# Two iota tables of a graph layer's one-hots, read by VectorE from PSUM instead of SBUF

## The chip, the cores and the metric

The kernel runs on one core of a Trainium2 chip. The metric is the device time of one execution in microseconds (us). Engines are named as in the profile: PE (TensorE matmuls), PEld (TensorE weight loads), DVE (VectorE), ACT (ScalarE), POOL (GpSimd), SP (SyncE). SBUF is the on-chip working memory, PSUM the accumulator memory that TensorE writes.

## The reference

There are 12,500 nodes with 128 features each, 200,000 edges sorted by destination, and four edge types. All tensors are float32.

```python
h = jnp.maximum(_layernorm(x, axis=-1), 0.0)
xs = h[src]
for i in range(4):
    msgs = msgs + jnp.where((edge_types == i)[:, None], xs @ W[i] + b[i], 0.0)
out = x + jax.ops.segment_sum(msgs, dst, num_segments=12500)
```

The destinations are drawn as 12500 times the square of a uniform number, so low nodes receive more edges than high ones. Because the edges are sorted, a run of 1,024 consecutive edges falls on few tiles of 128 nodes.

## The kernel before

**The table.** In the first stage (98 tiles of 128 nodes) the kernel normalizes x, applies relu, transposes on PE (L656), multiplies by all four weight matrices at once (L665), lets DVE add the bias (L524, which reads ps_y from PSUM and bias from SBUF), and stores the 128x512 result to a table in HBM (L280). A row of 128 numbers of that table is the message of one (node, type). The stage also transposes the index lists into columns: table_row (which row of the table an edge needs) and dst_col (its destination as a float). `ps_i`, one PSUM bank, takes these transposes.

**Early edges.** While the table is made, POOL gathers the raw x rows of the first 15,360 edges with 120 indirect DMAs of 128 rows (L330) into early_x. The list of rows is read from src_col in SBUF.

**The main loop.** The edges are cut into superblocks of 8 columns of 128 edges. After the table is complete, POOL gathers messages for the other superblocks with 1,443 indirect DMAs of 128 rows (L338, `gather`, called at L345). Each reads its 128 row numbers from row_stage in SBUF, which ACT fills (L407) when PE has released one of four slots (L715). POOL runs through these gathers in order and does nothing else.

For each superblock and each node tile that it touches (a pair; 294 in all) DVE makes one-hot matrices in two halves of four columns (L593): an entry is 1 where node_iota + tile_base[j] equals the edge's destination. The loop bounds come from memory (L229). PE multiplies the one-hots with the messages (L710) into ps_sum, and DVE adds the previous pair's sum to acc (L585, acc from SBUF, ps_sum from PSUM). There is one onehot buffer of two halves, so DVE may write a half again only when PE has read it (half_free, L592); PE waits for onehot_ready (L708) and for the slot's gathers (L705).

Once in nine superblocks an early one is worked off (`early=True`): DVE then also makes four one-hots of node and type together, 128x1024 each (L603, from key_iota, tile_base and key_col; the profile names their target y, whose memory they use), and PE sums normalized features by type (L737) and counts (L728) and multiplies by the weights (L746). The order of superblocks is fixed by the program: eight from the table, then one early, 15 times, then the rest.

Both `scalar_tensor_tensor` calls have three inputs: a tensor in0 (the iota), a tensor in1 (the edges' column, repeated along the nodes), and a number for each partition (tile_base) that also lies in SBUF. node_iota is 128x128 and key_iota 128x512, both made by POOL at the start (L312, L316).

Of the kernel before, what the change touches and what calls it, by code (L numbers as in the profile page):

```python
# [29 lines left out]
P = 128  # L30
# [11 lines left out]
def gnn_program(nc, x, src, dst, etype, w, b, out, table):  # L42
# [3 lines left out]
    ydim = n_types * d  # L46
# [21 lines left out]
    def sb(name, shape, dt=F32):  # L68
        return nc.alloc_sbuf_tensor(name, shape, dt)

    def ps(name, shape):
        return nc.alloc_psum_tensor(name, shape, F32)

    def sem(name):
        return nc.alloc_semaphore(name)
# [6 lines left out]
    node_iota = sb("node_iota", [P, P])  # L82
    tile_base = sb("tile_base", [P, node_tiles])
    key_iota = sb("key_iota", [P, n_types, P])
# [60 lines left out]
    ps_y = ps("ps_y", [P, 2, 512])  # L145
    ps_sum = ps("ps_sum", [P, 2, 512])
    ps_i = ps("ps_i", [P, 4, P])

    loaded_src0 = sem("loaded_src0")
    loaded_first = sem("loaded_first")  # L150
# [7 lines left out]
    own_steps = sem("own_steps")  # L158
    pads_set = sem("pads_set")
    dve_consts = sem("dve_consts")  # L160
    early_f_ready = sem("early_f_ready")
    early_transposed = sem("early_transposed")
    early_cols = sem("early_cols")
# [54 lines left out]
    def halves(tiles):  # L218
        return (0, -(-tiles // 2)), (-(-tiles // 2), tiles)
# [6 lines left out]
    def load_range(eng, s):  # L226

        regs = [eng.alloc_register(f"{eng.engine.name}_{n}_{nc.next_id()}") for n in ("lo", "hi")]
        eng.reg_load(regs, flat_ranges[0:1, bass.ds(s * 4, 2)])  # L229
        return (eng.snap(regs[0], min_val=0, max_val=node_tiles - 1),  # L230
                eng.snap(regs[1], min_val=1, max_val=node_tiles), regs)
# [14 lines left out]
    with nc.Block() as block:  # L246
# [198 lines left out]
        def _(dve):  # L445
# [88 lines left out]
            for m, op in enumerate((ALU.min, ALU.max)):  # L534
# [18 lines left out]
            dve.wait_ge(consts, 8)  # L553
            nc.vector.scalar_tensor_tensor(out=key_col[:, :], in0=type_col[:, :], scalar=float(type_step),
                                           in1=dst_col[:, 0, 0:early_tiles], op0=ALU.mult, op1=ALU.add).then_inc(own_steps, 1)
            dve.wait_ge(own_steps, 8)
            dve.wait_ge(ranges_ready, 16)
            for k in range(Y_SLOTS):
# [8 lines left out]
            nc.vector.tensor_reduce(store_after[:, :], last_touch[:, :, :], AX.X, ALU.max).then_inc(store_after_ready, 1)  # L567
            dve.wait_ge(early_gathered, 16 * early_tiles)
            dve.sem_inc(key_onehot_free, 2)

# [7 lines left out]
            def add_sums(q):  # L580
                tile = tile_before()
                dve.wait_ge(pair_added, q + 1)
                dve.wait_ge(half_free, q * 2 + 2)
                at = flat_acc[:, bass.ds(tile * d, d)]
                return nc.vector.tensor_tensor(at, at, ps_sum[:, bass.ds((q + 1) % 2, 1), 0:d], ALU.add)  # L585

            def superblock(s, tiles, early=False):
                lo, hi, regs = load_range(dve, s)
                with dve.Fori(lo, hi) as j:
                    q = count()  # L590
                    for half, (a, z) in enumerate(halves(tiles)):
                        dve.wait_ge(half_free, q * 2 + (half + 1))  # L592
                        nc.vector.scalar_tensor_tensor(  # L593
                            out=onehot[:, a:z, :],
                            in0=node_iota[:, :].unsqueeze(1).broadcast_to([P, z - a, P]),
                            scalar=tile_base[:, bass.ds(j, 1)],
                            in1=flat_dst[:, bass.ds(s * SB_TILES + a, z - a)].unsqueeze(2).broadcast_to([P, z - a, P]),
                            op0=ALU.add, op1=ALU.is_equal).then_inc(onehot_ready, 1)
                    if early:
                        p = early_count()  # L600
                        for u in range(tiles // 2):
                            dve.wait_ge(key_onehot_free, p * (tiles // 2) + (u + 1))
                            nc.vector.scalar_tensor_tensor(  # L603
                                out=key_onehot[:, u % 2, :, :],
                                in0=key_iota[:, :, :].rearrange("p t n -> p (t n)").unsqueeze(1).broadcast_to([P, 2, ydim]),
                                scalar=tile_base[:, bass.ds(j, 1)],
                                in1=key_col[:, bass.ds(s * SB_TILES + 2 * u, 2)].unsqueeze(2).broadcast_to([P, 2, ydim]),
                                op0=ALU.add, op1=ALU.is_equal).then_inc(key_onehot_ready, 1)
                        dve.reg_add(p_reg, p_reg, 1)
                    add_sums(q).then_inc(pair_added, 1)  # L610
                    dve.reg_mov(before_reg, j)
                    dve.reg_add(q_reg, q_reg, 1)

                dve.wait_ge(pair_added, count() + 1)
                dve.sem_inc(sbs_passed, 1)
                for r in regs:
                    dve.free_register(r)

            with dve.Fori(0, EARLY_SBS) as i:
                s = EARLY_SBS + i * (EARLY_ROUNDS * SLOTS)  # L620
                superblock(s, SB_TILES)

                for t in range(SB_TILES):
                    nc.vector.bn_stats(e_stats[:, t, :], flat_early[:, bass.ds((i * SB_TILES + t) * d, d)]).then_inc(e_stats_taken, 1)
                dve.wait_ge(e_stats_taken, (i + 1) * SB_TILES)
                dve.wait_ge(e_used, i + 1)
                nc.vector.tensor_tensor(
                    type_mask[:, :, 0:n_types], node_iota[:, 0:n_types].unsqueeze(1).broadcast_to([P, SB_TILES, n_types]),
                    type_col[:, bass.ds(i * SB_TILES, SB_TILES)].unsqueeze(2).broadcast_to([P, SB_TILES, n_types]),
                    ALU.is_equal).then_inc(e_mask_ready, 1)  # L630
                for t in range(SB_TILES):
                    nc.vector.bn_aggr(e_mean_var[:, t, :], e_stats[:, t, :]).then_inc(e_mean_var_ready, 1)
                superblock(s + 1, SB_TILES)
                dve.wait_ge(e_std_ready, i + 1)
                nc.vector.reciprocal(e_rstd[:, :], e_std[:, :]).then_inc(e_rstd_ready, 1)
                dve.wait_ge(e_rstd_ready, i + 1)
                nc.vector.scalar_tensor_tensor(out=e_shift[:, :], in0=e_mean_var[:, :, 0], scalar=-1.0,
                                               in1=e_rstd[:, :], op0=ALU.mult, op1=ALU.mult).then_inc(e_norm_ready, 1)
                for m in range(2, EARLY_ROUNDS * SLOTS):
                    superblock(s + m, SB_TILES)  # L640
                superblock(i, SB_TILES, early=True)
# [150 lines left out]
```

## Time and profile before

| | |
|---|---|
| Runs | 2638.77 us median of 3 (2616.4, 2638.77, 2645.23) |
| Span of the profiled execution, first to last instruction | 2029.2 us |
| Median less that span | 609.6 us |
| POOL busy | 1536.1 us, 76% |
| PE busy | 1116.0 us, 55% |
| DVE busy | 714.7 us, 35% |
| ACT busy | 169.6 us, 8% |

The span is that of one profiled execution. Its time around the span is not listed by itself, so the median less the span stands for it. Busy time counts instructions that run on an engine's data path; waits, branches and the issue of DMAs by a queue are not in it, but an indirect DMA on POOL is an instruction of POOL, since POOL makes its descriptors. "Idle before" is the time in which an engine stood still ahead of an instruction, with what ended it; "issue" means that nothing the profile shows held it.

### The profile page before, as it was taken

To read this page: it belongs to the slowest core of one execution; us is meant where nothing else is said; L and a number is where in the kernel's file an instruction comes from. 1 tells how busy PE (TensorE), PEld (TensorE's weight loads), DVE (VectorE), ACT (ScalarE), POOL (GpSimd) and SP (SyncE) were. 2 spreads that over 40 slices of the span, in tenths; PEclk is the share of its full clock that TensorE was granted. 3 is DMA by queue.
4 is the path that set the end of the run, shared out by engine and by line. 5 is a ranking of instruction groups with operands and counts; after the bars stand their busy time and mean duration, and the time that the engine had idled before them with its cause. 6 is when DMAs were issued, how large, how long until landed. Compare 5 with 4: busy or idle time off the path is not lost.

```text
span 2029.2 us, 24251 instructions
## 1 busy us (share of the span) xinstructions
PE 1116.0 (55%) x5394; PEld 930.4 (46%) x5395; DVE 714.7 (35%) x1589; ACT 169.6 (8%) x565; POOL 1536.1 (76%) x1575
## 2 busy tenths in 40 slices
PE   6952545456564554654646556456555555554555
PEld 2322444344454444544535455445544444444554
DVE  6862223132332332433424334243322222232333
ACT  4530011010010100101001001010000000000000
POOL 7777777777777777777777777777777777777775
PEclk9985767776665776767878767787777777787788
DMA  9962221212122112211212121211312222212222
GB/s 305 328 206 54 51 52 50 53 49 52 51 50 52 50 49 52 51 51 49 50 52 50 50 52 50 51 50 50 104 51 70 51 51 52 69 51 52 69 52 59
DMA packets 94959, 144.09 MB, mean 71 GB/s; under 512 B 27065, under 2 KB 57267, under 8 KB 94947
## 3 DMA queue, kind: packets, MB, share of 16 engines
q0 software_dynamic: 50016, 102.53, 19.8%
q1 hardware_dynamic: 40537, 39.02, 5.8%
q10 hardware_dynamic: 4394, 2.40, 0.4%
q8 instruction: 4, 0.07, 0.0%
q14 instruction: 8, 0.07, 0.0%
HBM read 111.76 MB, written 32.09 MB: 71 GB/s over the span
## 4 chain that ended last, share of the span: by engine, by line
POOL 70%; issue 24%; PE 3%; DMA 1%; POOLq 1%; DVE 0%; ACT 0%; DVEq 0%; ACTq 0%; PEldq 0%
POOL messages L338 65%; POOL early_x L330 6%; PE ps_sum L710 2%; DMA messages<-message_table,row_stage 1%; PE ps_y L737 1%; PE ps_y L728 0%; POOLq L342 0%; POOLq L344 0%; DMA src_rows<-in_src 0%; PE ps_sum L746 0%; POOLq L345 0%; DVE onehot L593 0%; POOLq L246 0%; ACT row_stage L407 0%; DVE acc L585 0%
## 5 line engine op out<-in xcount | busy, mean ns | idle before, releaser
L338 POOL DMA_INDIRECT messages<-message_table,row_stage x1443 | 1420.5, 984 | 439.7 <-issue 437.9
L710 PE MATMUL ps_sum<-messages,onehot 128*128 128x128 f32 x4438 | 843.4, 370 | 852.9 <-DMA messages<-message_table,row_stage 769.7
L710 PEld LDWEIGHTS ps_sum<-messages,onehot 128*128 128x128 f32 x4438 | 791.0, 277 | 904.5 <-issue 890.5
L593 DVE SCALAR_TENSOR_TENSOR onehot<-node_iota,tile_base,dst_col 128x512 f32<-128x512 f32 x586 | 431.1, 749 | 1234.2 <-PE ps_sum L710 1147.0
L407 ACT COPY row_stage<-table_row 128x8 int32 (+2 forms) x181 | 35.7, 198 | 1602.5 <-PEq L715 1597.8
L330 POOL DMA_INDIRECT early_x<-in_x,src_col x120 | 113.5, 946 | 41.6 <-issue 39.4
L665 PE MATMUL ps_y<-w_sb,h_t 128*128 128x512 f32 x196 | 104.7, 626 | 4.6 <-DVE y L524 4.3
L737 PE MATMUL ps_y<-y 128*128 128x512 f32 x240 | 106.8, 598 | 0.0
L603 DVE SCALAR_TENSOR_TENSOR y<-key_iota,tile_base,key_col 128x1024 f32<-128x1024 f32 x60 | 75.9, 1285 | 35.5 <-PE ps_y L737 35.5
L585 DVE TENSOR_TENSOR acc<-acc,ps_sum x294 | 82.1, 279 | 2.3 <-PE ps_sum L710 2.1
L524 DVE TENSOR_TENSOR y<-ps_y,bias 128x512 f32<-128x512 f32 x98 | 66.9, 684 | 16.5 <-PE ps_y L665 11.4
L737 PEld LDWEIGHTS ps_y<-y 128*128 128x128 f32 x240 | 42.8, 193 | 53.5 <-issue 36.3
L372 ACT ACTIVATE h<-acc,shift,rstd 128x128 f32 (+1 forms) x97 | 48.3, 498 | 0.6 <-DVE shift L473 0.2
L425 ACT ACTIVATE y<-early_x,e_shift,e_rstd 128x128 f32 x120 | 48.1, 484 | 0.0
L665 PEld LDWEIGHTS ps_y<-w_sb,h_t 128*128 128x128 f32 x196 | 29.7, 191 | 36.4 <-issue 33.6
L728 PE MATMUL ps_y<-onehot,type_mask 128*128 128x128 f32 x240 | 35.9, 311 | 18.9 <-DVE onehot L593 18.9
L728 PEld LDWEIGHTS ps_y<-onehot,type_mask 128*128 128x128 f32 x240 | 32.8, 219 | 22.4 <-DVE onehot L593 22.4
L656 PE MATMUL ps_t<-ident,h 128*128 128x128 f32 x98 | 27.7, 284 | 11.7 <-ACT h L384 9.8
L656 PEld LDWEIGHTS ps_t<-ident,h 128*128 128x128 f32 x98 | 14.0, 143 | 39.8 <-issue 26.2
L746 PEld LDWEIGHTS ps_sum<-w_sb,bias 128*128 128x128 f32 x120 | 14.5, 191 | 30.2 <-issue 30.2
L397 ACT COPY h_t<-ps_t 128x128 f32<-128x128 f32 x98 | 25.8, 263 | 30.1 <-PE ps_t L656 29.4
L746 PE MATMUL ps_sum<-w_sb,bias 128*128 128x128 f32 x120 | 17.3, 287 | 17.9 <-ACT edge_counts L435 17.9
(63 smaller groups left out, 147.5 us busy)
## 6 DMA issues: line engine op xcount, KB each, us to landing
message_table<-y SPq DMA_DIRECT2D x98, 256.0 KB
messages<-message_table,row_stage POOLq DMA_INDIRECT x1443
out<-acc SPq DMA_DIRECT2D x6, 896.0 KB
acc<-in_x SPq DMA_DIRECT2D x4, 896.0 KB, 7.5
early_x<-in_x,src_col POOLq DMA_INDIRECT x120
acc<-in_x ACTq DMA_DIRECT2D x2, 896.0 KB, 10.3
acc<-in_x SPq DMA_DIRECT2D x1, 832.0 KB, 6.9
src_rows<-in_src SPq DMA_DIRECT2D x1, 640.0 KB
```

The source lines that it names most:

```text
L330: pool.indirect_dma_start(early_x[:, t, :], None, x, bass.IndirectOffsetOnAxis(ap=src_col[:, t:t + 1], axis=0)).then_inc(early_gathered, 16)
L338: pool.indirect_dma_start(messages[:, k, t, :], None, table_rows, bass.IndirectOffsetOnAxis(ap=row_stage[:, k, t:t + 1], axis=0)).then_inc ...
L372: nc.scalar.activation(h[:, k, :], flat_acc[:, bass.ds(n * d, d)], ACT.Relu, bias=flat_shift[:, bass.ds(n, 1)], scale=flat_rstd[:, bass.ds ...
L425: nc.scalar.activation(e_h[:, t, :], flat_early[:, bass.ds((i * SB_TILES + t) * d, d)], ACT.Relu, bias=e_shift[:, t:t + 1], scale=e_rstd[: ...
L524: nc.vector.tensor_tensor(y[:, i % Y_SLOTS, :], ps_y[:, i % 2, :], bias[:, :], ALU.add).then_inc(y_ready, 1)
L585: return nc.vector.tensor_tensor(at, at, ps_sum[:, bass.ds((q + 1) % 2, 1), 0:d], ALU.add)
L593: nc.vector.scalar_tensor_tensor(out=onehot[:, a:z, :], in0=node_iota[:, :].unsqueeze(1).broadcast_to([P, z - a, P]), scalar=tile_base[:, ...
L603: nc.vector.scalar_tensor_tensor(out=key_onehot[:, u % 2, :, :], in0=key_iota[:, :, :].rearrange("p t n -> p (t n)").unsqueeze(1).broadcas ...
L665: nc.tensor.matmul(ps_y[:, i % 2, :], h_t[:, i % 2, :], w_flat, start=True, stop=True).then_inc(y_done, 1)
L710: ins = nc.tensor.matmul(ps_sum[:, bass.ds(q % 2, 1), 0:d], onehot[:, t, :], messages[:, k, t, :], start=(t == 0), stop=(t == tiles - 1))
L728: ins = nc.tensor.matmul(ps_y[:, 1, 0:P], type_mask[:, t, :], onehot[:, t, :], start=(t == 0), stop=(t == SB_TILES - 1))
L737: ins = nc.tensor.matmul(ps_y[:, 0, :], e_h[:, 2 * u + t, :], key_onehot[:, u % 2, t, :], start=(u == 0 and t == 0), stop=(u == SB_TILES / ...
```

## The change

Two PSUM tensors are filled once, ahead of the main loop, with copies of node_iota and key_iota: `ps_node` is new, and `ps_key` is another name for the bank `ps_i`, whose last reader (the copy of type_col, L550) stands before it on DVE. The one-hots of L593 and L603 read in0 from there. The other two inputs, the output, the shapes and the order stay. `type_mask` (L627) still reads node_iota from SBUF.

```diff
--- before.py
+++ after.py
@@ -145,6 +145,8 @@
     ps_y = ps("ps_y", [P, 2, 512])
     ps_sum = ps("ps_sum", [P, 2, 512])
     ps_i = ps("ps_i", [P, 4, P])
+    ps_node = ps("ps_node", [P, P])
+    ps_key = ps_i[:, :, :].rearrange("p t n -> p (t n)")
 
     loaded_src0 = sem("loaded_src0")
     loaded_first = sem("loaded_first")
@@ -158,6 +160,7 @@
     own_steps = sem("own_steps")
     pads_set = sem("pads_set")
     dve_consts = sem("dve_consts")
+    iotas_in_psum = sem("iotas_in_psum")
     early_f_ready = sem("early_f_ready")
     early_transposed = sem("early_transposed")
     early_cols = sem("early_cols")
@@ -553,6 +556,8 @@
             dve.wait_ge(consts, 8)
             nc.vector.scalar_tensor_tensor(out=key_col[:, :], in0=type_col[:, :], scalar=float(type_step),
                                            in1=dst_col[:, 0, 0:early_tiles], op0=ALU.mult, op1=ALU.add).then_inc(own_steps, 1)
+            nc.vector.tensor_copy(ps_node[:, :], node_iota[:, :]).then_inc(iotas_in_psum, 1)
+            nc.vector.tensor_copy(ps_key, key_iota[:, :, :].rearrange("p t n -> p (t n)")).then_inc(iotas_in_psum, 1)
             dve.wait_ge(own_steps, 8)
             dve.wait_ge(ranges_ready, 16)
             for k in range(Y_SLOTS):
@@ -567,6 +572,7 @@
             nc.vector.tensor_reduce(store_after[:, :], last_touch[:, :, :], AX.X, ALU.max).then_inc(store_after_ready, 1)
             dve.wait_ge(early_gathered, 16 * early_tiles)
             dve.sem_inc(key_onehot_free, 2)
+            dve.wait_ge(iotas_in_psum, 2)
 
 
 
@@ -592,7 +598,7 @@
                         dve.wait_ge(half_free, q * 2 + (half + 1))
                         nc.vector.scalar_tensor_tensor(
                             out=onehot[:, a:z, :],
-                            in0=node_iota[:, :].unsqueeze(1).broadcast_to([P, z - a, P]),
+                            in0=ps_node[:, :].unsqueeze(1).broadcast_to([P, z - a, P]),
                             scalar=tile_base[:, bass.ds(j, 1)],
                             in1=flat_dst[:, bass.ds(s * SB_TILES + a, z - a)].unsqueeze(2).broadcast_to([P, z - a, P]),
                             op0=ALU.add, op1=ALU.is_equal).then_inc(onehot_ready, 1)
@@ -602,7 +608,7 @@
                             dve.wait_ge(key_onehot_free, p * (tiles // 2) + (u + 1))
                             nc.vector.scalar_tensor_tensor(
                                 out=key_onehot[:, u % 2, :, :],
-                                in0=key_iota[:, :, :].rearrange("p t n -> p (t n)").unsqueeze(1).broadcast_to([P, 2, ydim]),
+                                in0=ps_key.unsqueeze(1).broadcast_to([P, 2, ydim]),
                                 scalar=tile_base[:, bass.ds(j, 1)],
                                 in1=key_col[:, bass.ds(s * SB_TILES + 2 * u, 2)].unsqueeze(2).broadcast_to([P, 2, ydim]),
                                 op0=ALU.add, op1=ALU.is_equal).then_inc(key_onehot_ready, 1)
```

## Rows read from the trace of the kernel before

**Rows 1.** The page: span, busy time by engine, and the chain that ended last

```profile
span 2029.2 us, 24251 instructions
PE 1116.0 (55%) x5394; PEld 930.4 (46%) x5395; DVE 714.7 (35%) x1589; ACT 169.6 (8%) x565; POOL 1536.1 (76%) x1575
...
POOL 70%; issue 24%; PE 3%; DMA 1%; POOLq 1%; DVE 0%; ACT 0%; DVEq 0%; ACTq 0%; PEldq 0%
```

**Rows 2.** Waits: engine, tile and line, releaser: us in total, times, longest

```profile
DVE onehot L593 <- PE ps_sum L710: 1147.0, 432, 9.2
...
PE ps_sum L710 <- DMA messages<-message_table,row_stage: 769.7, 140, 37.9
POOL messages L338 <- issue: 437.9, 1437, 0.3
...
POOL messages L338 <- ACT row_stage L407: 1.8, 6, 0.3
```

**Rows 3.** Groups by line, POOL: count | busy us, mean ns | idle before

```profile
L338 POOL DMA_INDIRECT messages<-message_table,row_stage x1443 | 1420.5, 984 | 439.7 <-issue 437.9 <-ACT row_stage L407 1.8
```

**Rows 4.** Single lines, L338 and L330: durations in ns, minimum/median/maximum

```profile
L338 POOL DMA_INDIRECT messages<-message_table,row_stage x1443: 940/944/1554, 158.3 to 2017.3; - x181
...
L330 POOL DMA_INDIRECT early_x<-in_x,src_col x120: 940/944/1103, 5.1 to 157.1; - x120
```

**Rows 5.** Timeline, main loop: start us, us, engine, line

```profile
1433.07 1.22 POOL L338 DMA_INDIRECT messages<-message_table,row_stage  x1 [0.30 <-issue]
...
1437.09 1.42 POOL L338 DMA_INDIRECT messages<-message_table,row_stage  x1 [0.30 <-issue]
...
1432.73 0.75 DVE L593 SCALAR_TENSOR_TENSOR onehot<-node_iota,tile_base,dst_col 128x512 f32<-128x512 f32 x1 [0.77 <-PE ps_sum L710]
...
1436.28 1.41 DVE L593 SCALAR_TENSOR_TENSOR onehot<-node_iota,tile_base,dst_col 128x512 f32<-128x512 f32 x2 [2.61 <-issue]
```

**Rows 6.** Timeline, an early superblock: a gather beside L603

```profile
907.35 2.48 DVE L603 SCALAR_TENSOR_TENSOR y<-key_iota,tile_base,key_col 128x1024 f32<-128x1024 f32 x2
907.89 1.55 POOL L338 DMA_INDIRECT messages<-message_table,row_stage  x1 [0.30 <-issue]
```

**Rows 7.** Timeline, table stage: an early gather beside L524

```profile
65.24 0.94 POOL L330 DMA_INDIRECT early_x<-in_x,src_col  x1 [0.30 <-issue]
...
64.41 1.42 DVE L524 TENSOR_TENSOR y<-ps_y,bias 128x512 f32<-128x512 f32 x2
```

**Rows 8.** Groups by line and shape, DVE: count | busy us, mean ns | idle before

```profile
L593 DVE SCALAR_TENSOR_TENSOR onehot<-node_iota,tile_base,dst_col 128x512 f32<-128x512 f32 x584 | 430.3, 751 | 1232.8 <-PE ps_sum L710 1145.5 <-issue 54.0 <-PE ps_sum L748 31.9
L603 DVE SCALAR_TENSOR_TENSOR y<-key_iota,tile_base,key_col 128x1024 f32<-128x1024 f32 x60 | 75.9, 1285 | 35.5 <-PE ps_y L737 35.5
L524 DVE TENSOR_TENSOR y<-ps_y,bias 128x512 f32<-128x512 f32 x98 | 66.9, 684 | 16.5 <-PE ps_y L665 11.4 <-DMA message_table<-y 4.6
...
L593 DVE SCALAR_TENSOR_TENSOR onehot<-node_iota,tile_base,dst_col 128x128 f32<-128x128 f32 x1 | 0.3, 350 | 0.2 <-PE ps_sum L710 0.2
...
L554 DVE SCALAR_TENSOR_TENSOR key_col<-type_col,dst_col 128x120 f32<-128x120 f32 x1 | 0.3, 282 | 0.0
```

**Rows 9.** Groups by line and shape, the late stretch 1420 to 2018 us

```profile
L338 POOL DMA_INDIRECT messages<-message_table,row_stage x466 | 456.7, 980 | 142.0 <-issue 141.7 <-ACT row_stage L407 0.3
...
L710 PE MATMUL ps_sum<-messages,onehot 128*128 128x128 f32 x1750 | 314.3, 354 | 286.2 <-DMA messages<-message_table,row_stage 276.7 <-issue 2.7 <-DVE onehot L593 2.5
...
L585 DVE TENSOR_TENSOR acc<-acc,ps_sum x109 | 30.4, 279 | 0.0
```

**Rows 10.** Timeline, between table stage and main loop, and the end

```profile
135.03 0.28 DVE L554 SCALAR_TENSOR_TENSOR key_col<-type_col,dst_col 128x120 f32<-128x120 f32 x1
...
136.15 2.92 DVE L564 SCALAR_TENSOR_TENSOR y<-ranges,order 1x196 f32<-1x196 int32 x7 [0.84 <-DMA ranges<-ranges_by_chunk]
...
161.47 1.41 DVE L593 SCALAR_TENSOR_TENSOR onehot<-node_iota,tile_base,dst_col 128x512 f32<-128x512 f32 x2 [20.80 <-issue]
...
2017.31 0.95 POOL L338 DMA_INDIRECT messages<-message_table,row_stage  x1 [0.30 <-issue]
```

## The prediction

> **What bounds the kernel now.** I read the page first: POOL is busy for 76% of the span, PE for 55%, DVE for 35%, and the chain that ended last lies on POOL for 70% and on "issue" for 24% [rows 1]. The waits say what that issue is: 437.9 us in 1,437 pieces of at most 0.3 us ahead of the gathers of L338, so POOL's own pause between two gathers. Only 1.8 us of POOL's idle time waited for a list of rows from ACT, while PE waited 769.7 us for gathered data and DVE 1147.0 us for PE [rows 2]. From 158.3 us to the start of the last gather at 2017.3 us the kernel runs at the pace at which POOL issues gathers, and the end follows about 11 us later (2029.2 less 2018.3, where the last gather ends) [rows 1, 10]. DVE and PE have spare time; what counts is what they do to POOL.
>
> The third view, the durations of that one line, shows it. The gathers are all alike (128 rows of 512 bytes), the minimum is 940 ns and the median 944 ns, yet the maximum is 1554 [rows 4] and the mean 984 [rows 3]. Something stretches a minority. The timeline shows what. The gather at 1433.07 took 1.22 us, and the one-hot of L593 that ran beside it ended at 1432.73 + 0.75 = 1433.48. The gather at 1437.09 took 1.42 us; of the two one-hots in a row beside it, 1.41 us in all, the end is at 1436.28 + 1.41 = 1437.69 [rows 5]. End of the one-hot, less start of the gather, less the gather's excess over 0.944: 0.41 - 0.28 = 0.13 us and 0.60 - 0.48 = 0.12 us. So each gather reaches, some 0.12 us after its start, a point that it does not pass while that one-hot runs; after it everything takes the usual 0.82 us. L603 does the same to the gather at 907.89, which took 1.55 us [rows 6]: the first of its two instructions ends near 907.35 + 1.28 = 908.63, and 0.74 - 0.61 = 0.13. A gather reads its 128 row numbers from SBUF, and both one-hots read two SBUF tensors, the iota and the edge column.
>
> **Whether one PSUM input frees POOL.** The row for that is L524, whose in0 is in PSUM and in1 (bias) in SBUF, the arrangement that the change gives to L593 and L603. It takes 67 us of the table stage [rows 8], beside the early gathers, which also read row numbers from SBUF. The gather at 65.24 passes its point at 65.36 while two L524 run until 64.41 + 1.42 = 65.83, and takes 0.94 us; with the stretch above it would have taken 1.41 [rows 7]. In all 120 early gathers the median is 944 and the maximum 1103 [rows 4], although L524 covers about 67 of their 153 us. So the stretch goes with two SBUF tensors, not with any DVE work. What L524 lacks is the third input: tile_base, one number per partition, also from SBUF. No row has one SBUF tensor with such a number, so this stays the main doubt (a rival below).
>
> **The change, part by part.**
> (1) Gathers. Removed: 1443 x (984 - 944) = 57.7 us [rows 3, 4]. All of it is on the chain, since POOL is never idle but for its 0.3 us pauses. Bounds: nothing, if the third input keeps the stretch, and 1443 x (984 - 940) = 63.5, if every gather became the fastest. I take 57.7, because L524's neighbours show the median as their usual duration. A few two-input instructions are left (L627, L637); they are short and rare.
> (2) The one-hot's own duration. A one-hot takes 751 ns for 512 columns and 350 for 128 [rows 8], so (751 - 350) / 384 = 1.04 ns a column and 217 ns fixed. L554, the same operation with a constant instead of tile_base, has 282 - 125 = 157 fixed; tile_base so costs 60 ns. L524, 512 columns with one PSUM input, takes 684. Estimate for the new form: 684 + 60 = 744, no change. Bounds: 684 ns below, and above 1285, the price of 1024 columns now, if PSUM gave a column only every second cycle [rows 8]. I take 744, for L524 reads PSUM at the full rate while PE writes other banks. The Trainium skill, "VectorE: DVE Perf Modes", section on the TRN2 errata, speaks against the change: it gives VectorE 58 cycles plus the columns from SBUF and 120 from PSUM. By that, an estimate from the page, each one-hot would be 62 cycles or 65 ns longer, 42 us of DVE time over 644; L524's row, no longer than a two-SBUF form, does not show it. By either, the sum here hides it under POOL: in the late stretch PE still waits 276.7 us for gathers in 109 pairs, 2.5 us a pair [rows 9], and a pair has two one-hots. Even at the upper bound, 2 x 0.53 = 1.07 us fit in there. Without that cover a pair would pay those 1.07 us, 315 us in 294 pairs.
> (3) The two copies. 512 columns for about L524's 684 ns and 128 for about L554's 282, together 1.0 us (bounds 0.5 and 1.6, half of it and L603's 1285 with the 128-column one-hot's 350). They stand behind L554, which ends at 135.31; DVE then waits 0.84 us for the ranges anyway, and after L564 and its reduce it idles 20.80 us before the first one-hot at 161.47, until the early gathers have landed [rows 10]. Behind them on DVE are only L564 and the table for the output stores, used some 100 us later. The added wait for both copies stands behind the wait for the early gathers. Cost: zero. If that cover were gone, 1 us. No copy or wait is put on POOL, SP, ACT or PE, and no DMA is moved.
> (4) What is late next. Still POOL: 944 + 304 (437.9 / 1437) = 1.25 us a gather. Rows come early: the longest wait of POOL for ACT is 0.3 us [rows 2]. At 8 gathers a superblock, POOL's new pace is 9.98 us; in the late stretch (466 gathers, 58 superblocks, 109 pairs [rows 9]) PE's 314.3 us are 5.4 us a superblock. PE keeps up, and its waits shrink.
> Sum: -57.7 + 0 + 0. The profiled span would be 2029.2 - 57.7 = 1971.5 us. With the 609.6 us around it the profiled execution stands, as far as can be told, at the median, so 2638.8 - 57.7 = 2581 us, 2.2% less. The three runs lie from 22 us below the median to 6 above; taking 1% as the least that can be told from no change is taking 26 us.
>
> **Rivals.**
> *A. The stretch stays* (the change does not do what it is thought to). tile_base is a second SBUF input, and if POOL's read is shut out by any two of them, nothing moves: 2639 us. For it: no row excludes it. Against: the number is one column, and its visible price is 60 ns; if it shut POOL out only for those, the stretch per hit would fall to under a tenth. A middle case, half of the stretch left, gives 2610.
> *B. DVE becomes the bound.* The place is the pair: one-hot half, four matmuls, half free. If PSUM gave the repeated 128-column iota at a quarter of the rate, a one-hot would take 0.22 + 4 x 0.53 = 2.35 us instead of 0.75, two of them 3.2 us more in a pair. PE's wait of 2.54 us a pair, less what POOL saves (57.7 / 294 = 0.20), covers 2.34; 0.86 us x 294 = 253 us are left, and the time is 2581 + 253 = 2834. It decides from 0.75 + 2.34 / 2 = 1.9 us a one-hot. Against: L524 reads 512 columns in 684 ns; for: L524's PSUM columns are all different, and no row rereads the same 128.
> *C. The gain is there and something else takes part of it*: gathers in closer order land later, or PE waits more at the early superblocks, where its work is longest. The 1.8 us of POOL's waiting [rows 2] would grow; at 20 us the time is 2601.
>
> **How the numbers follow.** Forecast 0.72; A 0.11 (and its middle case 0.05); B 0.03; C 0.09. The predicted time is the forecast's, 2581. Its own range is the sum's bound of 63.5 and the runs' spread, 2555 to 2602. C and half of the middle case belong into 8 in 10, so the high end goes to 2615; the low end stays at 2555. Faster by over 1% (below 2612) takes the forecast, C and half of the middle case: 0.83. Within 1%: A and the rest, 0.14. Slower: 0.03.
>
> **What would show it right or wrong.** Right: L338's mean falls from 984 to about 945 with the median unchanged and a maximum near 1100; its busy time falls from 1420.5 to about 1363; the pauses stay at 304 ns; POOL's wait for ACT stays under 5 us; the one-hots stay within 684 to 820 ns; PE's wait for gathers falls below 770 us; the last gather starts near 1960. A: mean at 984 and gathers that still end a fixed time after a one-hot. B: one-hots of 1.9 us and more, and POOL waiting for row_stage. C: the mean falls and the wait of POOL for ACT grows. The forecast is wrong in its frame if the span falls by 58 us and the runs do not.

## The result

The changed kernel takes 2667.12 us (median of 4, 2656.13 to 2669.64), the kernel before 2627.59 us beside it (median of 4, 2614.0 to 2645.23). The ratio is 1.0193, 95% interval 1.0137 to 1.0249: slower by 1.9%, where 2.2% faster was forecast.

The page of the changed kernel, to be held against [rows 1]:

```profile
span 2667.7 us, 24253 instructions
PE 1224.0 (46%) x5394; PEld 995.8 (37%) x5395; DVE 717.6 (27%) x1591; ACT 169.1 (6%) x565; POOL 1476.9 (55%) x1575
...
another core or an unknown queue 40%; PE 24%; issue 21%; DVE 7%; DVEq 7%; PEld 1%; ACT 0%; DMA 0%; ACTq 0%; PEldq 0%; SPq 0%
```

The span is 638.5 us longer than in the profile of before, although POOL is busy for 59 us less and the chain no longer lies on POOL. This execution took 2669.64 us in all, 2 us more than its span. So there are no 600 us around a span here, and the profiled execution of before must have been another case than the runs that were listed beside it; e1 below tests that. Its groups answer to [rows 3] and [rows 8]:

```profile
L341 POOL DMA_INDIRECT messages<-message_table,row_stage x1443 | 1361.4, 943 | 1125.5 <-ACT row_stage L410 668.5
...
L599 DVE SCALAR_TENSOR_TENSOR onehot<-ps_node,tile_base,dst_col 128x512 f32<-128x512 f32 x586 | 434.4, 749 | 1652.7 <-remote 938.1
...
L609 DVE SCALAR_TENSOR_TENSOR y<-ps_i,tile_base,key_col 128x1024 f32<-128x1024 f32 x60 | 75.1, 1279 | 125.2 <-remote 83.5
```

The durations of the gathers, as [rows 4] had them:

```profile
L341 POOL DMA_INDIRECT messages<-message_table,row_stage x1443: 938/944/961, 265.9 to 2643.4; - x181
```

Every stretched gather is gone: the longest takes 961 ns and took 1554. The one-hots keep their duration (for 512 columns 750 ns and before 751, for 1024 columns 1279 and 1285; the 749 above also counts two smaller ones). But the gathers begin at 265.9 us instead of 158.3 and end 626 us later than they did. The waits, beside [rows 2], say where the time is:

```profile
ACT row_stage L410 <- PEq L721: 1607.5, 131, 30.4
...
DVE onehot L599 <- remote: 938.1, 151, 20.0
POOL messages L341 <- ACT row_stage L410: 668.5, 84, 108.5
PE ps_sum L716 <- DVE onehot L599: 506.4, 114, 14.7
POOL messages L341 <- issue: 457.0, 1359, 3.4
```

POOL waited 1.8 us for lists of rows, now 668.5. "remote" is a release that no recorded event explains. A stretch of the timeline shows what such a wait is:

```profile
1033.80 2.05 PE L716 MATMUL ps_sum<-messages,onehot 128*128 128x128 f32 x16 [1.53 <-issue]
...
1035.11 0.75 DVE L599 SCALAR_TENSOR_TENSOR onehot<-ps_node,tile_base,dst_col 128x512 f32<-128x512 f32 x1 [1.74 <-issue]
...
1040.42 0.75 DVE L599 SCALAR_TENSOR_TENSOR onehot<-ps_node,tile_base,dst_col 128x512 f32<-128x512 f32 x1 [4.57 <-remote]
1040.50 0.20 ACT L410 COPY row_stage<-table_row 128x8 int32 x1 [7.82 <-PEq L721]
```

PE ends its last matmul at 1035.85. DVE waits for that matmul's semaphore (half_free) and goes on at 1040.42; ACT, which gets its release through PE, at 1040.50. The signal is about 4.5 us late, and both stand still for it while POOL goes on gathering. It is so in the table stage too, which the change does not touch. Here are ACT's copies of the transposes there:

```profile
32.80 0.27 ACT L400 COPY h_t<-ps_t 128x128 f32<-128x128 f32 x1 [7.74 <-issue]
...
40.50 0.27 ACT L400 COPY h_t<-ps_t 128x128 f32<-128x128 f32 x1 [7.05 <-remote]
...
49.60 0.27 ACT L400 COPY h_t<-ps_t 128x128 f32<-128x128 f32 x1 [8.44 <-issue]
```

In the profile of before, such copies follow each other at about 1 us there. I call these **late signals**. The same trace shows what they go with. POOL's last early gather starts at 156.4 us. Of the 98 copies of this line, 18 start between 20 and 170 us, while gathers run or have just ended, and 76 in the 95 us behind that, when POOL issues none (one at 183.33 us, for example, and the next at 184.38).

In the profile of before the early gathers run just as close together, and all 98 copies are made by 129.5 us. So dense gathers alone do not make signals late everywhere; in this execution they are late while gathers are issued.

### The profile page after: what moved, and what is told of

Read it like the earlier page. It is cut to its first block, busy times and chain, and to the rows that moved or that the text cites. A ratio compares the mean times of both kernels' runs of the same rounds, so it can differ in the third digit from the quotient of the medians.

```text
span 2667.7 us, 24253 instructions
## 1 busy us (share of the span) xinstructions
PE 1224.0 (46%) x5394; PEld 995.8 (37%) x5395; DVE 717.6 (27%) x1591; ACT 169.1 (6%) x565; POOL 1476.9 (55%) x1575
## 4 chain that ended last, share of the span: by engine, by line
another core or an unknown queue 40%; PE 24%; issue 21%; DVE 7%; DVEq 7%; PEld 1%; ACT 0%; DMA 0%; ACTq 0%; PEldq 0%; SPq 0%
PE ps_sum L716 16%; DVE onehot L599 3%; PE ps_y L671 3%; PE ps_y L743 3%; DVEq L232 2%; DVE acc L591 2%; DVEq L591 1%; DVEq L599 1%; PEld ps_sum L716 1%; PE ps_sum L752 1%; DVE y L609 1%; PE ps_y L734 1%; DVEq L595 1%; DVE y L527 0%
## 5 line engine op out<-in xcount | busy, mean ns | idle before, releaser
L341 POOL DMA_INDIRECT messages<-message_table,row_stage x1443 | 1361.4, 943 | 1125.5 <-ACT row_stage L410 668.5
L716 PE MATMUL ps_sum<-messages,onehot 128*128 128x128 f32 x4438 | 890.3, 381 | 1143.0 <-DVE onehot L599 506.4
L716 PEld LDWEIGHTS ps_sum<-messages,onehot 128*128 128x128 f32 x4438 | 822.8, 286 | 1209.6 <-issue 1056.7
L599 DVE SCALAR_TENSOR_TENSOR onehot<-ps_node,tile_base,dst_col 128x512 f32<-128x512 f32 x586 | 434.4, 749 | 1652.7 <-remote 938.1
L671 PE MATMUL ps_y<-w_sb,h_t 128*128 128x512 f32 x196 | 123.3, 725 | 98.3 <-issue 96.2
L743 PE MATMUL ps_y<-y 128*128 128x512 f32 x240 | 125.3, 678 | 62.7 <-DVE y L609 62.7
L609 DVE SCALAR_TENSOR_TENSOR y<-ps_i,tile_base,key_col 128x1024 f32<-128x1024 f32 x60 | 75.1, 1279 | 125.2 <-remote 83.5
L743 PEld LDWEIGHTS ps_y<-y 128*128 128x128 f32 x240 | 51.1, 229 | 127.3 <-DVE y L609 73.2
L734 PE MATMUL ps_y<-onehot,type_mask 128*128 128x128 f32 x240 | 54.6, 419 | 80.7 <-DVE onehot L599 53.9
L734 PEld LDWEIGHTS ps_y<-onehot,type_mask 128*128 128x128 f32 x240 | 50.4, 319 | 84.6 <-DVE onehot L599 56.8
```

The lines of the kernel that those rows point to most:

```text
L341: pool.indirect_dma_start(messages[:, k, t, :], None, table_rows, bass.IndirectOffsetOnAxis(ap=row_stage[:, k, t:t + 1], axis=0)).then_inc ...
L599: nc.vector.scalar_tensor_tensor(out=onehot[:, a:z, :], in0=ps_node[:, :].unsqueeze(1).broadcast_to([P, z - a, P]), scalar=tile_base[:, ba ...
L609: nc.vector.scalar_tensor_tensor(out=key_onehot[:, u % 2, :, :], in0=ps_key.unsqueeze(1).broadcast_to([P, 2, ydim]), scalar=tile_base[:, b ...
L671: nc.tensor.matmul(ps_y[:, i % 2, :], h_t[:, i % 2, :], w_flat, start=True, stop=True).then_inc(y_done, 1)
L716: ins = nc.tensor.matmul(ps_sum[:, bass.ds(q % 2, 1), 0:d], onehot[:, t, :], messages[:, k, t, :], start=(t == 0), stop=(t == tiles - 1))
L734: ins = nc.tensor.matmul(ps_y[:, 1, 0:P], type_mask[:, t, :], onehot[:, t, :], start=(t == 0), stop=(t == SB_TILES - 1))
```

## The experiments

All kernels here share one edit of SP's stores, which loads the seven store points one by one:

```diff
-            regs = [sp.alloc_register(f"sp_store_after_{n}") for n in range(len(STORE_TILES))]
-            sp.reg_load(regs, store_after[0:1, :])
...
-                sp.wait_ge(sbs_passed, sp.snap(reg, min_val=0, max_val=full_sbs + 1) + 1)
+                after = sp.value_load(store_after[0:1, n:n + 1], min_val=0, max_val=full_sbs + 1)
+                sp.wait_ge(sbs_passed, after + 1)
```

**e1, the kernel before with that edit.**

> The kernel before, with one edit that all experiments here carry: SP loads its seven store points one at a time, just ahead of each wait, instead of all at once. Theory L (late signals): the profile of before was an exceptional execution. Ordinary executions of both kernels hold pauses in which a finished matmul's semaphore reaches DVE, ACT and PE several us late, about 600 us in all. Then this run is 2600 to 2650 us, its profile shows a span within 5 us of its time, POOL waiting for ACT's row_stage for some 500 to 700 us, and hundreds of us of late signals; L338's mean is still 960 to 985 ns. Theory P (pace of POOL, as predicted): the profile shows a span near 2030 again and POOL without waits, and some 600 us lie outside the span in every run.

Measured: 2606.63 us; the kernel before beside it 2605.9 us (23 runs); ratio 1.0051 [1.0013, 1.0089]. Span and waits:

```profile
span 2638.2 us, 24271 instructions
...
DVE onehot L592 <- remote: 899.7, 156, 19.4
POOL messages L337 <- ACT row_stage L406: 578.0, 73, 108.0
```

Theory L holds. The kernel before, run again, has late signals as well; the profile that the prediction read had none. Gathers: mean 992 ns, so the stretch is there too.

**e2, the changed kernel with that edit.**

> The changed kernel with the same edit of SP. Theory L: 1.4% to 2.5% slower than before as measured, 2655 to 2675 us, and POOL's gathers at 943 ns. If the 1.9% were a matter of one chip or of the code's exact place, it shrinks below 1%.

Measured: 2657.35 us, ratio 1.0235 [1.0187, 1.0283]. The loss repeats; POOL's wait for ACT is 659.5 us.

**e3, copies only.** The one-hots read SBUF, the two copies stay:

```diff
-                            in0=ps_node[:, :].unsqueeze(1).broadcast_to([P, z - a, P]),
+                            in0=node_iota[:, :].unsqueeze(1).broadcast_to([P, z - a, P]),
...
-                                in0=ps_key.unsqueeze(1).broadcast_to([P, 2, ydim]),
+                                in0=key_iota[:, :, :].rearrange("p t n -> p (t n)").unsqueeze(1).broadcast_to([P, 2, ydim]),
```

> The changed kernel, but L593 and L603 read node_iota and key_iota from SBUF again; the two copies into PSUM stay. Theory R (the reads from PSUM cost the 1.9%, by sharing PSUM with TensorE's writes): same as before, within 0.5%, near 2630, gathers' mean back at 980. Theory F (the faster gathers cost it, through what they trigger): also same as before. Theory S (the set-up costs it: two instructions more, another length of code): 1.5 to 2% slower, near 2667.

Measured: 2610.61 us, ratio 1.0062 [1.0024, 1.0100], the same as e1; in its profile POOL waits 524.5 us for ACT. The set-up costs nothing that shows (theory S falls); the loss comes with the reads.

**e4, only L593's reads from PSUM**: e3's second pair of lines alone.

> The changed kernel, but L603 reads key_iota from SBUF; L593 (586 of 646 one-hots) reads PSUM. Theory R and F: nine tenths of the change, 1.5 to 2% slower than before. If the 128x1024 reads of L603 are what costs, in the early superblocks where PE is busiest, it is within 0.5% of before.

Measured: 2651.18 us, ratio 1.0205 [1.0156, 1.0254]; gathers' mean 958 ns. Nearly the whole loss comes with L593's reads.

**What the late signals go with.** In each trace I took the waits of DVE ahead of a one-hot of L593 (half_free) on which it stood idle for over 0.1 us, the distance from the end of the last matmul before it to DVE's start, and the number of gathers that POOL had started in the 20 us up to that matmul's end. In e1, 10 or 11 gathers: 112 waits, median 0.18 us; 12 or 13: 209, median 0.18 us (mean 1.7); 14 or 15: 78, median 3.1 us; 16 or 17: 12 waits, median 13.4 us. The other three are alike. In the profile of before, 16 or 17 gathers stand ahead of 241 waits, with a median of 0.15 us. So in e1 to e4 lateness goes with POOL's pace, and the next experiments change the pace.

**e5 to e8, pauses of POOL.** Ahead of gathers POOL clears a small tile (w columns); e5 does it once for a superblock (its `t % 8` and `t // 8` stand where the others have 1), the others for each gather:

```diff
+                    if first is not None and t % 1 == 0:
+                        pool.wait_ge(paused, first + t // 1)
+                        pool.sem_inc(slots_taken, 1)
+                        pool.memset(pause[:, :], 0.0).then_inc(paused, 1)
                     pool.indirect_dma_start(
```

e5 (changed kernel, 256 columns a superblock):

> The changed kernel with a pause of POOL ahead of each superblock's eight gathers: a memset of 128x256 and its semaphores, about 0.35 us, which is what the one-hots' stretch gave to POOL before (8 x 0.04 us). In the profiles of e1 to e4 a PE signal is the later the more gathers were issued in the 20 us before it: median 0.04 us up to 13 gathers, 3 us with 14 or 15, 11 us and more with 16. Theory F (the faster gathers cost the 1.7% between e1 and e2, since they make signals later): back near e1, 2600 to 2625 us. Theory R (reading PSUM while PE writes it costs it): stays at e2's 2657 us or above.

Measured: 2685.49 us, ratio 1.0303 [1.0249, 1.0357]. Theory F's return to 2600 does not come. Its lump ahead of eight gathers leaves them as dense among themselves, so it does not settle the matter of pace. It is 28 us slower than e2, which nothing here explains.

e6 (before, 64 columns a gather):

> The kernel before with a pause of POOL of some 0.15 to 0.25 us ahead of each gather (memset of 128x64), a pace near 1.45 us a gather instead of 1.29. Theory D (density): signals come on time when gathers are spaced, since each gather's 16 completions then no longer pile up; the late signals shrink and the kernel becomes bound by POOL at 170 + 1443 x 1.45 = 2260 to 2400 us, far faster than before. Against it (late signals belong to the chip's state, whatever the pace): 2606 plus up to 290 us, 2700 or more.

Measured: 2572.9 us, ratio 0.9790 [0.9707, 0.9873]. A slower POOL makes a faster kernel, by 2.1%, but not by what D hoped: the memset partly hid under the gathers (mean distance of two gathers 1.35 us, not 1.45), and signals stayed late.

e7 (changed, 64 columns a gather):

> The changed kernel with the same pause. Theory D with F: with signals on time POOL bounds, so the stretch that the change removes counts again, and it is 30 to 60 us faster than e6. Theory R: the PSUM reads cost 1.7% here too, so slower than e6 by some 40 us, or equal where the two offset.

Measured: 2672.12 us, ratio 1.0259 [1.0189, 1.0330], slower than e6 by 99 us. Signals are late in both, so the condition of D with F is not met; theory R has the sign, at more than twice its size.

e8 (before, 256 columns a gather):

> The kernel before with a pause near 0.35 us ahead of each gather (128x256), a pace near 1.62 us. Theory D: no late signals beyond those of the table stage; bound by POOL, 170 + 1443 x 1.62 = 2500 us (2450 to 2560), so slower than e6 and still faster than before. Against D: 2750 or more.

Measured: 2455.46 us, ratio 0.9421 [0.9359, 0.9484], 5.8% faster than the kernel before. Its waits:

```profile
DVE onehot L599 <- PE ps_sum L716: 1355.9, 354, 10.8
PE ps_sum L716 <- DMA messages<-message_table,row_stage: 1032.0, 152, 18.3
...
POOL pause L342 <- ACT row_stage L413: 106.9, 1, 106.9
```

and its groups:

```profile
L343 POOL DMA_INDIRECT messages<-message_table,row_stage x1443 | 1446.2, 1002 | 260.5 <-POOL pause L342 168.2 <-issue 92.3
...
L342 POOL MEMSET pause<- 128x256 f32 x1440 | 472.1, 328 | 107.8 <-ACT row_stage L413 106.9
```

The picture of [rows 2] is back: PE waits for gathered data, the "remote" waits of DVE have left the top of the list, and POOL waits only once, 106.9 us at the end of the table stage. The time follows as there: first gather at 264.6 us, 1443 gathers at 1.51 us, 2439 us. Theory D expected 2450 to 2560 and its rival 2750 or more: spacing the gathers makes the signals come on time here. For a kernel whose one-hots read SBUF the change comes between 1.35 us (e6) and 1.49 us a gather (e8).

**e9 to e12, meant to tell PSUM reads from the lost stretch.** Behind each one-hot DVE runs one more instruction with an unused result: e9 and e10 in e3's kernel, e11 and e12 in the changed one.

```diff
                             op0=ALU.add, op1=ALU.is_equal).then_inc(onehot_ready, 1)
+                        dve.wait_ge(junk_done, q * 2 + (half + 1))
+                        dve.sem_inc(junk_steps, 1)
+                        nc.vector.bn_stats(junk[:, :], key_iota[:, :, :].rearrange("p t n -> p (t n)")).then_inc(junk_done, 1)    # e9, e11
+                        nc.vector.bn_stats(junk[:, :], ps_key).then_inc(junk_done, 1)           # e10
+                        nc.vector.tensor_tensor(junk[:, :], key_iota[:, :, :].rearrange("p t n -> p (t n)"), key_iota[:, :, :].rearrange("p t n -> p (t n)"), ALU.add).then_inc(junk_done, 1)  # e12
```

> Control of e10: the one-hots read SBUF as before (and two SBUF tensors, so they stretch gathers), and behind every one-hot of L593 DVE runs one more instruction with a single input: statistics over 512 columns of key_iota in SBUF, about 0.65 us, 588 in all, result unused. DVE has idle time for it: within 1% of e3 (2610), or slower by what 1.3 us of DVE a pair adds to the turn of one-hot and matmuls; only the difference to e10 counts.

> As e9, but the added statistics read the copy of key_iota in PSUM: 588 reads of 512 columns of PSUM on top, the one-hots as before, the gathers stretched as before. Theory R (reading PSUM beside PE's writes delays PE's signals and costs the 1.7%): slower than e9 by 1 to 2%, 25 to 50 us. Theory T (it is the missing lock-out of POOL's reads, not PSUM, that costs): equal to e9 within 0.5%.

> The changed kernel (one-hots read PSUM, gathers unstretched) with e9's added instruction, one SBUF input, no stretch of gathers. Control of e12. Theories R and T: slower than e9 by 1.5 to 2%, as e2 is against e3.

> The changed kernel; behind each one-hot DVE adds two SBUF tensors of 512 columns (0.69 us, result unused), which brings the lock-out of POOL's reads back: gathers' mean near 980 ns again, while the one-hots still read PSUM. Theory T: the loss goes, at least 1.5% faster than e11 and near e9. Theory R: equal to e11 within 0.5%, or slower by the stretch.

These four ran on another chip, and there the kernel before took 2030.12 us (17 runs). Measured: e9 2036.8 us, ratio 1.0038 [1.0023, 1.0053]; e10 2038.01, 1.0048 [1.0030, 1.0066]; e11 1971.45, **0.9714 [0.9694, 0.9734]**; e12 2044.33, 1.0069 [1.0049, 1.0090]. So whether signals are late depends on where the kernel runs, and the profile of before, with its span of 2029.2 us, came from a case like this one. Here the forecast is right. Span and gathers of e9, then of e11:

```profile
span 2034.6 us, 25446 instructions
...
L343 POOL DMA_INDIRECT messages<-message_table,row_stage x1443 | 1426.5, 989 | 439.7 <-issue 438.5 <-ACT row_stage L412 1.2
```

```profile
span 1973.6 us, 25446 instructions
...
L343 POOL DMA_INDIRECT messages<-message_table,row_stage x1443 | 1365.0, 946 | 440.0 <-issue 436.0 <-ACT row_stage L412 4.0
L602 DVE SCALAR_TENSOR_TENSOR onehot<-ps_node,tile_base,dst_col 128x512 f32<-128x512 f32 x586 | 437.0, 746 | 843.4 <-PE ps_sum L722 724.9 <-issue 94.1 <-PE ps_sum L760 23.0
```

The gathers give back 61.5 us of POOL, the span 61.0 and the median 65.35, and little else moves: POOL's pause is 0.3 us in both, its wait for ACT at most 4 us in all. e12 against e11 is the reverse test. The added instruction has two SBUF inputs in e12 and one in e11, and takes 686 and 684 ns. With two, the kernel takes 73 us more:

```profile
L343 POOL DMA_INDIRECT messages<-message_table,row_stage x1443 | 1435.6, 995 | 439.8 <-issue 438.5 <-ACT row_stage L412 1.2
```

POOL's gathers grow by 70.6 us, and each of the 302 that are over 0.06 us longer than the median ends a fixed 0.82 us (within 0.04) after one of the added instructions ended. The added instruction of e12 also writes 512 columns where that of e11 writes 6; but e11's one-hots write 512 columns too, and no gather beside them is stretched. An added instruction with a single input costs at most 7 us (e9 against the kernel before). e10 against e9: 586 more reads of 512 columns of PSUM beside PE's writes cost nothing clear of noise where signals come on time.

**e13 to e15** ran on a third chip, with late signals (kernel before 2624.14 us, 11 runs).

> The changed kernel as in e2. Where the kernel before takes about 2030 us (signals on time): 2031 - 58 = 1973 us, 2.9% faster, L338's counterpart at 944 ns, as predicted. Where it takes about 2610 us (late signals): 2657 us, 1.8% slower, as in e2.

Measured: 2673.5 us, ratio 1.0168 [1.0123, 1.0213]; the loss once more.

e14 is e8's pause in the changed kernel:

> The changed kernel with e8's pause ahead of each gather (1.45 us a gather instead of e8's 1.51). Signals on time: bound by POOL, 170 + 1443 x 1.45 = 2265 us. Late placement: if the change only ever acts through POOL's pace and 1.45 still spaces the completions enough, 2455 - 82 = 2373 us; if 1.45 is already too dense (e6 at 1.41 took 2573), 2500 to 2600; if reading PSUM itself delays signals, more than 2600.

Measured: 2532.57 us, ratio 0.9617 [0.9568, 0.9666]; e8 had 0.9421. Neither 2373 nor above 2600. Waits and gathers:

```profile
DVE onehot L605 <- remote: 715.8, 186, 10.6
...
POOL pause L345 <- ACT row_stage L416: 240.4, 32, 108.3
...
L346 POOL DMA_INDIRECT messages<-message_table,row_stage x1443 | 1372.2, 951 | 269.3 <-issue 176.2 <-POOL pause L345 93.1
```

Late signals return. The gathers are 51 ns shorter than e8's, which may be enough; but the one-hots also read PSUM here and SBUF in e8, and the two ran on different chips, so the record does not say which of these brings them back.

> As e12: one-hots read PSUM, an added two-SBUF-input instruction behind each brings the lock-out of POOL back. Late placement: theory T (the missing lock-out costs) 2600 to 2630 us, like e1; theory R (reads of PSUM cost) 2650 us or more, like e2. Signals on time: 2044 us as in e12.

Measured: 2712.6 us, ratio 1.0329 [1.0286, 1.0372]. Theory T expected 2600 to 2630 and gets no support; theory R's 2650 or more is met. But the added instruction also lengthens DVE's part of each pair, and no control for that ran on such a chip.

**e16 to e18** are e9, e10 and e11 again, meant as those controls; they ran on a fourth chip, where signals are on time (before 2031.73 us, 11 runs).

> As e9 (one-hots read SBUF, lock-out of POOL as before, one added single-input DVE instruction reading SBUF behind each one-hot). Late placement: the added 0.69 us stands in the turn of one-hot and matmul, so 1 to 2% slower than before: ratio 1.01 to 1.02. Signals on time: 1.004 as in e9.

> As e10, the added instruction reads PSUM. Late placement: theory R (reads of PSUM delay signals) at least 1% slower than e16; if it equals e16 within 0.5%, PSUM reads as such cost nothing, and the loss hangs on POOL's gathers coming closer together. Signals on time: equal to e16.

> As e11 (one-hots read PSUM, no lock-out, added single-input instruction). Late placement: theory T (the missing lock-out costs) slower than e15's ratio of 1.033, or at least 1.5% slower than e16; with theory R alone it equals e15. Signals on time: 0.971 as in e11.

Measured: ratios 1.0048 [1.0032, 1.0064], 1.0044 [1.0029, 1.0059] and 0.9708 [0.9694, 0.9721]. They confirm e9 to e11 and leave the question of e15 open.

**All paces together**, on the chips with late signals. Pace is the mean distance between the starts of two gathers in the profiled execution, without the distances over 3 us, in which POOL waited:

| run | one-hots read | pace us | profiled execution us | median us | ratio to before |
|---|---|---|---|---|---|
| changed kernel | PSUM | 1.276 | 2670 | 2667 | 1.0193 |
| e13 | PSUM | 1.276 | 2680 | 2674 | 1.0168 |
| e2 | PSUM | 1.277 | 2660 | 2657 | 1.0235 |
| e5 | PSUM | 1.287 | 2686 | 2685 | 1.0303 |
| e4 | PSUM (L593) | 1.289 | 2666 | 2651 | 1.0205 |
| e15, added instruction | PSUM | 1.293 | 2722 | 2713 | 1.0329 |
| e7 | PSUM | 1.307 | 2663 | 2672 | 1.0259 |
| e1 | SBUF | 1.322 | 2640 | 2607 | 1.0051 |
| e3 | SBUF | 1.324 | 2593 | 2611 | 1.0062 |
| e6 | SBUF | 1.349 | 2597 | 2573 | 0.9790 |
| e14 | PSUM | 1.446 | 2537 | 2533 | 0.9617 |
| e8 | SBUF | 1.493 | 2452 | 2455 | 0.9421 |

Where the one-hots read SBUF, the time falls as the gathers are spaced. Where they read PSUM, it does not follow the pace below 1.31 us, and falls only in e14.

Measured as above, waits in which DVE started over 2 us after the matmul's end: 152 in e1 with 934 us in all, 150 in e2 with 918, 143 in e6 with 992, 164 in e14 with 740, 5 in e8 with 18, and 7 each in e9 (46 us) and e11 (44), which gather every 1.29 and 1.25 us on a chip with signals on time. So the sum tells the two regimes apart, but not one late run from another: e6 has more of it than e1 and is faster.

Another difference of the late traces is PE's granted clock, 0.666 over the changed kernel's profile and 0.758 over that of before; PE's work takes 1224.0 us there and 1116.0 here. These 108 us are far less than the 638.5, and a slower matmul does not explain a DVE that goes on 4.5 us after its end. Which of the two brings the other was not tested.

## Why the prediction was wrong

**The step that failed is its frame**: "With the 609.6 us around it the profiled execution stands, as far as can be told, at the median". The step put 609.6 us outside the span; the runs show 2 us there (2667.7 and 2669.64 in the changed kernel, 2638.2 and 2640.11 in e1). The runs listed were, judging by e1, executions with late signals; the profile was one without. A bottleneck read from that trace, POOL, was applied to runs in which POOL stands waiting for 578 us (e1). The prediction had the warning in its own table, 600 us that nothing accounted for, and named the failure at its end ("the span falls by 58 us and the runs do not"), but gave it no chance of its own.

**Step 1, the gathers, was right in size, and wrong about the chain.** 1443 x (984 - 944) = 57.7 us was forecast for POOL. POOL's gathers fell by 61.5 us from e9 to e11, and by 76 us from e3 to e2 (1437.1 to 1361.2). On the chips with signals on time, that is the whole story: 2.9% faster, 58.7 us (e11) and 59.5 us (e18) under the kernel before, with one DVE instruction more behind each one-hot; the changed kernel by itself ran on no such chip. The main doubt, whether tile_base keeps the lock-out (the holding up of gathers beside a one-hot), is settled there: it does not. On the late chips the 76 us turned into waiting, and more: POOL's wait for ACT rose by 135 us, from 524.5 (e3) to 659.5 (e2). That the stretch ends at a fixed point holds beyond the three gathers that the prediction worked out: in the profile of before 183 gathers are over 0.06 us longer than the median, and each ends within 0.04 us of the end of an L593 or L603 plus 0.82 us.

**Step 2, the one-hot's duration: right.** 744 ns was estimated, 750 (changed kernel) and 746 (e11) measured. The Trainium skill's 62 more cycles for a PSUM source (VectorE: DVE Perf Modes, the section on the TRN2 errata) would have made it, by estimate, some 816; no run here shows them. The statistics added in e9 and e10 are the plainer test, one operation on 512 columns from either memory: 687 ns from SBUF and 692 from PSUM.

**Step 3, the copies: right.** 288 and 684 ns, 1.0 us forecast; e3 shows no cost clear of noise.

**Step 4, what is late next, failed with the frame.** "Still POOL" holds where signals are on time. In the timed runs it was PE's signal to DVE and ACT, and POOL waited for ACT for 668.5 us instead of the forecast's under 5.

**Rivals.** A and B did not occur. C has the sign of the mechanism ("gathers in closer order", POOL's wait for ACT growing) but expected part of the gain lost, not more than the gain.

**What stays open.** That the forecast gain did not come is accounted for by the late signals. Why the change costs 47 to 51 us net on the late chips (e2 against e3 and e1) is not settled. Two causes are left. The first is pace: the gathers come closer, and the spaced runs e6 and e8 are faster. Against it as the sole cause speaks the jump between e1 and e7 (65 us for 0.015 us of pace), three times and more what the steps from e1 to e6 and to e8 give, and that e5 and e15 are slower than e2 at a wider pace. The second is the reads of PSUM themselves: for it speak that jump and e15; e10 and e17 find no such cost, but only on chips with signals on time. The changed kernel with a pause that brings it to e8's 1.49 us would tell them apart, and was not run. Chip and hour changed together from one group of runs to the next, so whether it is the chip that decides on late signals is likely from four of them, but not shown. Where the delayed path lies, no run here shows.

## What to carry to other kernels

Before a bottleneck is read from a profile, its span must account for the listed times to a few us; a remainder of 600 us meant here that the profile showed another regime, and a forecast made on such a profile needs a chance for that. A saving on the engine that feeds DMAs is worth its size only while semaphores arrive on time; look for waits with no releaser, and for engines that restart several us after the matmul they wait for. There, spacing the producer can pay more than speeding it up: one memset of 128x256 ahead of each gather took 5.8% off (e8) on a chip with late signals. It is no cure for all chips: with POOL bound at 1.5 us a gather, 1443 gathers would take some 2160 us by themselves, where unspaced gathers at 1.25 us gave 1971 us in all (e11).

## What the runs showed of the hardware that was not expected

- Four chips ran the same kernel before at 2606 to 2624 us (two of them) and at 2030 to 2032 us (the other two), with narrow spreads on the second kind (2023.67 to 2037.31 in 17 runs).
- On the first kind DVE went on up to 10 us and more after the end of the last matmul before it (12 waits with a median of 13.4 us in e1), and spacing the gathers took this away: waits of over 2 us fell from 934 us in all at 1.32 us a gather (e1) to 18 us at 1.49 (e8).
- An indirect DMA on POOL is held at a point about 0.12 us after its start while a DVE instruction with two SBUF tensor inputs runs (all 183 stretched gathers of the profile of before, all 302 of e12). With one input in PSUM and a number per partition from SBUF it is not held: longest gather 961 ns over 1443. The Trainium skill, "SBUF — State Buffer", section "Who interferes with whom", says that a DVE instruction with two SBUF inputs contends with a GpSimd instruction that reads SBUF; e11 and e12 agree, at 946 and 995 ns a gather.
